# Softmax attention: maxima six pairs of heads ahead of the scores, their row fetched earlier and in one transfer

## The chip, the cores and the metric

The kernel runs on one core of one Trainium2 chip. The metric is the device time of one execution in microseconds. Three runs of the kernel before gave 2570.91, 2579.21 and 2582.12 us, median 2579.21 us. TensorE is called PE here, VectorE DVE, ScalarE ACT, GpSimd POOL and SyncE SP.

## The reference, cut to what matters

The program is four blocks, each added to the residual stream: softmax attention over the channels, a mixture of 8 experts, linear attention, and causal attention with a mixture of 16 experts. Only the first block is touched. There `x` and `ctx` are 64 sequences of 64 rows by 256 positions, cut into 32 tiles of two sequences.

```python
# _L0_xattn_ref, b = batch, 8 heads of 8 channels, 256 positions
q = split_heads(_proj(x, Wq, bq)); k = split_heads(_proj(c, Wk, bk)); v = split_heads(_proj(c, Wv, bv))
q = _apply_rotary(q_emb, q); k = _apply_rotary(k_emb, k)
scores = jnp.einsum('bhtc,bhsc->bhts', q, k) / math.sqrt(K_CH)
p_attn = jax.nn.softmax(scores, axis=-1)
out = jnp.einsum('bhts,bhsc->bhtc', p_attn, v)
```

## The kernel before, in words

`stage_softmax_attention` takes one tile per iteration of `for i in every`, and every engine has its own copy of that loop, in an order written out by hand; semaphores alone connect them. A tile has 16 heads (8 for each of its two sequences), worked on as 8 pairs, `k` = 0 to 7. Each pair needs two sets of products:

- Products for the maxima (`p_a`, L816). DVE reduces each of the pair's two heads to its largest score per query (`maxima`, L735), which goes into `top`.
- Scores themselves (`p_b`, L809), with the negative maximum taken off by an extra row (`SPLIT`, row 31 of each group of 32) of the same stationary block `rep`. ACT takes their exponential (L630).

`both(i, k)` (L791 to L819) issues the scores of pair `k` of tile `i` and, between them, the products for the maxima of a later pair. Before, that is four pairs on: pair `k + 4` of tile `i + 1` for `k` < 4, and pair `k - 4` of tile `i + 2` after that. Each half of `p_a` is written again only when DVE has reduced it (`a_done`), each half of `p_b` only when ACT has taken it (`prob_ready`).

Once all maxima of tile `i + 1` stand, PE turns them (L877) into `p_x[0]`, beside the v projection of tile `i + 3` (L881): call these six matmul records the turning block. ACT copies the turned row to `peak` (L664) and the values to `vaug` (L670), and SP sends the row to the four partitions 31, 63, 95 and 127 of `rep` (L543, four transfers). `both(i + 1, 0)` waits for them on `peak_in`.

Between the calls of `both` PE has other work: `project(i + 4, False)` after `k` = 0, `values(i - 1, 3)` and the router's `grade` (L211) after 1, `project(i + 4, True)` after 2, `values(i, 0)` after 3, the turning block after 4, `values(i, 1)` after 5, the output projection (L894) after 6, the router's `turn` (L193) and `values(i, 2)` after 7. `project` is L846 and L847; its True form waits for `cos_done`, that is for DVE's L721 on the False form. DVE's order is `maxima(i, 0)`, statistics of a later tile, `maxima(i, 1)`, rope with the cosines, `maxima` 2 and 3, rope with the sines, `maxima` 4 to 7, and then the reciprocal of the row sums (L782). The reciprocal waits for `pack_in`, the eight transfers of L592 that POOL issues.

SP's order in one iteration is: a blank store (L527), the twelve transfers that fill `rep` for tile `i + 3` (L504), the store of a finished tile (L537), the row of maxima (L543), loads (L518) and weights of the next stage (L402). The router works on tiles 0 to 15 only.

Of the kernel before, what the change touches and what calls it, by code (L numbers as in the profile page):

```python
# [20 lines left out]
PART = 128  # L21
# [18 lines left out]
def past(eng, sem, count):  # L40

    if not (isinstance(count, int) and count <= 0):
        eng.wait_ge(sem, count)
# [368 lines left out]
def stage_softmax_attention(nc, x_in, x_out, ctx, c):  # L412
# [15 lines left out]
    with st:  # L428
# [77 lines left out]
        with nc.Block() as block:  # L506
            @block.sync
            def _(sp):
                for dst, src in ((w_in, c["sa_w_in"]), (w_out, c["sa_w_out"]), (cos_t, c["sa_cos"]),
                                 (sin_t, c["sa_sin"]), (cols, c["sa_cols"]), (ident_f, c["ident"])):  # L510
                    sp.dma_start(dst[:], src).then_inc(const_in, 16)

                def load(m):
                    past(sp, xo_ready, LOAD * (m - 3))
                    past(sp, v_ready, LOAD * (m - 3))
                    at = slice(LOAD * (m % 4), LOAD * (m % 4) + LOAD)
                    for buf, src, done in ((xt, x_in, x_in_s), (ct, ctx, c_in_s)):
                        sp.dma_start(buf[:, at, :], src[LOAD * m:LOAD * (m + 1)].rearrange("t p d -> p t d")  # L518
                                     ).then_inc(done[m % 4], 16)

                load(0)
                load(1)
                route.load(sp)
                sp.wait_ge(zeroed, 2)
                for i in every:
                    if 0 <= i < len(blanks):
                        sp.dma_start(blanks[i].rearrange("(p r) d -> p (r d)", p=PART), blank[:]).then_inc(cleared[int(i >= CLEARS[0])], 16)  # L527
                    n = i + 3
                    if live(n):
                        sp.wait_ge(lo_ready, n + 1)  # L530
                        sp.wait_ge(hi_ready, n + 1)
                        sp.wait_ge(rep_init, min(n + 1, 4))
                        past(sp, b_ready, 2 * PAIRS * (n - 3))
                        fill_rows(sp, n, range(4 if n else 2))
                    if live(i - 3):
                        sp.wait_ge(xo_ready, i - 2)
                        sp.dma_start(x_out[i - 3], xo[:, (i - 3) % KEEP, :]).then_inc(stored[(i - 3) % KEEP], 16)  # L537
                    n = i + 1
                    if live(n):
                        sp.wait_ge(peak_ready, n + 1)  # L540
                        for j in range(4):
                            at = 32 * j + SPLIT
                            sp.dma_start(rep[at:at + 1, n % 4, :, 0:T].bitcast(fp32), peak[4 * j:4 * j + 4, n % 2, :].bitcast(fp32)  # L543
                                         ).then_inc(peak_in[n % 2], 16)
                    if (i + 9) % LOAD == 0 and 2 <= (i + 9) // LOAD < TILES // LOAD:
                        load((i + 9) // LOAD)
                    if i == 8:
                        held.load(sp)
                    if 0 <= i - 9 < held.RAWS:
                        held.load_raw(sp, c["L0_ffn_gate_proj"], c["L0_ffn_up_proj"], i - 9, i - 8)  # L550
                held.landed(sp)
                sp.wait_ge(route.wk_ready, route.TOP)
                sp.wait_ge(route.expert_ready, 1)
                for s in range(KEEP):
                    sp.wait_ge(stored[s], 16 * TILES // KEEP)
                sp.wait_ge(cleared[0], 16 * CLEARS[0])
                sp.wait_ge(cleared[1], 16 * (CLEARS[1] + MORE))
                sp.wait_ge(route.sent, 16 * route.n * route.TOP)
# [56 lines left out]
            def _(act):  # L615
# [23 lines left out]
                for i in every:  # L639
# [3 lines left out]
                    exp(i, 2)  # L643
                    keep(i - 1, 3)
                    exp(i, 3)
                    if routed(i - 6):
                        route.keep_scores(act, i - 6, 1, p_x[0][:, T:T + 8])
                    exp(i, 4)
                    keep(i, 0)
                    exp(i, 5)  # L650
                    n = i + 5
                    if live(n):
                        act.wait_ge(low_ready, n + 1)
# [2 lines left out]
                                       ).then_inc(xn_ready, 1)  # L656
                    if n in (0, 1, 2):
                        begin(n + 1)
                    n = i + 1
                    if live(n) or live(i + 3):  # L660
                        act.wait_ge(v_ready, i + 4)
                    if live(n):
                        past(act, peak_in[n % 2], 64 * (n // 2))
                        act.activation(peak[0:HEADS, n % 2, :], p_x[0][0:HEADS, T:2 * T], ACT.Copy).then_inc(peak_ready, 1)  # L664
                    n = i + 3
                    if live(n):
                        if n == 0:
                            act.wait_ge(zeroed, 5)
                        past(act, pv_done, GROUPS * (n - 3))
                        act.activation(vaug[:, n % 4, :, :, 0:KC].rearrange("p c h k -> p (c h) k"),  # L670
                                       p_x[0][:, 0:T].rearrange("p (n k) -> p n k", k=KC), ACT.Copy).then_inc(vaug_ready, 1)
                    exp(i, 6)
                    keep(i, 1)
                    exp(i, 7)
# [29 lines left out]
            def _(dve):  # L704
# [18 lines left out]
                                                 op0=ALU.add, op1=ALU.mult).then_inc(done, 1)  # L723

                def maxima(i, at):
                    n, k = (i + 1, at + 4) if at < 4 else (i + 2, at - 4)
                    if not live(n):
                        return
                    g, rows = pair(k ^ 1)
# [55 lines left out]
            def _(pe):  # L785
# [5 lines left out]
                def both(i, k):  # L791


                    n, m = (i + 1, k + 4) if k < 4 else (i + 2, k - 4)
                    if live(i) and k == 0:
                        pe.wait_ge(peak_in[i % 2], 64 * (i // 2 + 1))
                    if live(n) and m == 0:
                        pe.wait_ge(rep_in[n % 4], REP * (n // 4 + 1))
                    for h in range(2):
# [50 lines left out]
                for i in every:  # L850
# [1 line left out]
                    project(i + 4, False)  # L852
                    both(i, 1)
                    values(i - 1, 3)
                    if routed(i - 6):
                        route.grade(pe, i - 6, 1, p_x[0][:, T:T + 8], turned)

                    both(i, 2)
                    project(i + 4, True)
                    both(i, 3)  # L860
                    values(i, 0)

                    both(i, 4)
                    n, v = i + 1, i + 3
                    past(pe, vaug_ready, min(v, TILES))
                    past(pe, peak_ready, min(n, TILES))
                    past(pe, route.score_out, min(i - 5, ROUTED))
                    past(pe, route.ht_ready, min(i - 5, ROUTED))
                    if i > RANK:
                        pe.wait_ge(route.rank_out, 1)  # L870
# [11 lines left out]
                                           ct[:, v % RING, sc * PART:(sc + 1) * PART], w_in[:, 4, :], start=True, stop=True)  # L882
                    if mm is not None:
                        mm.then_inc(v_ready, 1)
                    both(i, 5)
                    values(i, 1)

# [8 lines left out]
                    if routed(i - 5) or i in (RANK, RANK + 1):  # L896
                        past(pe, vaug_ready, min(i + 4, TILES))
                        past(pe, peak_ready, min(i + 2, TILES))
                    if routed(i - 5):
                        route.turn(pe, i - 5, 1, p_x[0], ident_f[:])  # L900
                    if i == RANK:
# [1753 lines left out]
```

## Time and profile before

| | us |
|---|---|
| median of three runs | 2579.21 |
| the profiled execution | 2583.23 |
| span of that execution | 2581.4 |
| PE busy over the span | 2209.2 (86%) |
| DVE busy over the span | 1835.6 (71%) |
| ACT busy over the span | 1153.9 (45%) |

The span is 1.8 us shorter than the profiled execution. The first stage is the first 660 us of it. An instruction's row gives its start in us from the start of the span, how long it took, its engine, its line, its operation, what it writes and reads, how many are merged in the row, and in brackets how long the engine stood idle before it and what ended that idle time. One iteration runs from one first score product of pair 0 to the next. Idle time of an engine costs something only where the engines that set the end wait with it.

### The profile page before, as it was taken

Reading aid. Unit: us, or ns where it says so; the run is one execution under the profiler, and the core shown is the slowest. Engines: PE = TensorE matmul, PEld = TensorE weight load, DVE = VectorE, ACT = ScalarE, POOL = GpSimd, SP = SyncE. Lnnn points to the kernel's source line nnn. Section 1 sums busy time; section 2 is a strip of 40 time slices with the busy share of each in tenths; the row PEclk is TensorE's granted clock in tenths of the full one; section 3 lists DMA queues with packets and bytes.
Section 4 is the critical chain, followed back from the end, with each engine's and each line's share of the span. In section 5 each row is a group of like instructions: output and inputs, shape, how many; then the busy total and the mean of one; then the engine's idle time right before and its main releaser. Section 6 shows DMA issues by size and latency. Waiting matters only on the chain. (4 is left out here: it accounts for less than half of the span.)

```text
span 2581.4 us, 60448 instructions
## 1 busy us (share of the span) xinstructions
PE 2209.2 (86%) x20880; PEld 1675.0 (65%) x20880; DVE 1835.6 (71%) x3965; ACT 1153.9 (45%) x2509; POOL 1106.4 (43%) x1111
## 2 busy tenths in 40 slices
PE   6899888887678899994899998999988599999990
PEld 4555555543666677762677777777776477888880
DVE  4888888873546688765878878878787374545754
ACT  2776767665434333323444444444333264333330
POOL 3455554466144221002555445455487600334736
PEclk9988988886799999996999999999989799999995
DMA  5455554452359333312332332322334372445855
GB/s 114 120 124 137 147 136 129 104 144 85 120 171 296 110 107 120 92 58 53 82 89 57 83 84 60 85 73 69 81 96 116 129 253 82 136 141 182 264 172 148
DMA packets 250723, 313.10 MB, mean 121 GB/s; under 512 B 45248, under 2 KB 202944, under 8 KB 250432
## 3 DMA queue, kind: packets, MB, share of 16 engines
q1 hardware_dynamic: 189456, 219.11, 30.5%
q0 software_dynamic: 26624, 58.79, 8.3%
q10 hardware_dynamic: 34352, 31.34, 3.6%
q8 instruction: 180, 2.95, 0.5%
q14 instruction: 111, 0.91, 0.1%
HBM read 122.40 MB, written 102.24 MB: 87 GB/s over the span
## 5 line engine op out<-in xcount | busy, mean ns | idle before, releaser
L2136 POOL TENSOR_TENSOR ca_qk<-ca_qk,ca_q_swap 128x512 f32<-128x512 f32 x160 | 249.2, 1557 | 365.7 <-DVE ca_q_swap L2314 365.3
L735 DVE TENSOR_REDUCE soft_top<-soft_pa 128x2 fp32r<-128x512 f32 x512 | 327.9, 682 | 90.4 <-PE soft_pa L816 87.9
L630 ACT ACTIVATE soft_prob<-soft_pb 128x512 f32<-128x512 f32 x512 | 286.1, 594 | 180.9 <-PE soft_pb L809 179.1
L809 PE MATMUL soft_pb<-soft_rep 32*128 32x256 f32 x1024 | 207.5, 359 | 58.0 <-DVE soft_top L735 30.9
L809 PEld LDWEIGHTS soft_pb<-soft_rep 32*128 32x128 f32 x1024 | 135.0, 211 | 175.6 <-issue 81.3
L816 PE MATMUL soft_pa<-soft_rep 31*128 31x256 f32 x1024 | 217.4, 366 | 6.0 <-DVE soft_top L735 3.5
L1469 PE MATMUL moe_py<-moe_w_d,moe_at 128*128 x788 | 214.2, 387 | 1.5 <-issue 1.1
L1450 PE MATMUL moe_pgu<-moe_w_hi,moe_xt_hi 128*128 x472 | 192.9, 409 | 24.1 <-DVE moe_xt_lo L1362 13.4
L2406 PE MATMUL ca_py<-ca_w_hi,ca_ot_hi 128*128 128x256 f32 x512 | 155.8, 304 | 37.9 <-DVE ca_ot_lo L2335 37.8
L1368 DVE TENSOR_TENSOR moe_act_f<-moe_silu,moe_pgu 128x256 f32<-128x256 f32 (+1 forms) x236 | 88.6, 375 | 133.7 <-ACT moe_silu L1263 129.7
L2314 DVE TENSOR_TENSOR ca_q_swap<-ca_q_swap,ca_sin_q 128x512 f32<-128x512 f32 x128 | 116.8, 913 | 82.3 <-DMA ca_q_swap<-ca_q_f 81.9
L1263 ACT ACTIVATE moe_silu<-moe_pgu 128x256 f32<-128x256 f32 (+1 forms) x236 | 82.1, 348 | 203.9 <-PE moe_pgu L1450 203.7
L1450 PE MATMUL moe_pgu<-moe_w_hi,moe_xt_lo 128*128 x472 | 171.2, 363 | 0.0
L1450 PE MATMUL moe_pgu<-moe_w_lo,moe_xt_hi 128*128 x472 | 170.9, 362 | 0.0
L830 PE MATMUL soft_po<-soft_prob,soft_vaug 128*32 128x256 f32 x2048 | 164.0, 446 | 0.0
L2198 ACT ACTIVATE ca_ot_hi<-ca_po 128x512 fp32r<-128x512 f32 x128 | 69.5, 596 | 208.9 <-PE ca_po L2504 208.9
L2406 PE MATMUL ca_pp<-ca_ht_hi,ca_w_hi 128*128 128x512 f32 x312 | 138.2, 443 | 22.0 <-ACT ca_q_f L2184 18.4
L1184 POOL DMA_INDIRECT moe_yg<-moe_ys_rows,moe_held x112 | 115.8, 1034 | 87.7 <-DVE moe_ys L1375 38.5
L1362 DVE TENSOR_TENSOR moe_xt_lo<-moe_pt,moe_xt_hi 128x256 fp32r<-128x256 f32 x236 | 99.4, 421 | 72.8 <-ACT moe_xt_hi L1258 71.2
L2406 PE MATMUL ca_py<-ca_w_lo,ca_ot_hi 128*128 128x256 f32 x512 | 149.2, 291 | 0.0
L2406 PE MATMUL ca_py<-ca_w_hi,ca_ot_lo 128*128 128x256 f32 x512 | 149.1, 291 | 0.0
L364 POOL DMA_INDIRECT moe_rows<-moe_x_new,moe_held x80 | 78.1, 976 | 163.4 <-DVE moe_ys L1375 91.1
(377 smaller groups left out, 6265.7 us busy)
## 6 DMA issues: line engine op xcount, KB each, us to landing
ca_q_swap<-ca_q_f SPq DMA_DIRECT2D x640, 64.0 KB
moe_xs<-moe_rows SPq DMA_DIRECT2D x236, 128.0 KB, 2.1
soft_rep<-soft_parts SPq DMA_DIRECT2D x378, 64.0 KB
moe_rows<-soft_blank SPq DMA_DIRECT2D x27, 768.0 KB
moe_ys_rows<-moe_ys ACTq DMA_DIRECT2D x134, 128.0 KB
moe_ys<-moe_ys ACTq DMA_DIRECT2D x102, 128.0 KB
moe_xd<-scratch SPq DMA_DIRECT2D x64, 128.0 KB, 2.5
ca_vs<-ca_v SPq DMA_DIRECT2D x32, 256.0 KB, 3.9
```

What stands on the lines that cost most here:

```text
L630: act.activation(prob[:, k % 4, h, :], p_b[:, 2 * T * h:2 * T * (h + 1)], ACT.Exp).then_inc(prob_ready, 1)
L735: dve.tensor_reduce(heads[:, j, :, g], p_a[:, 2 * T * h:2 * T * (h + 1)].rearrange("p (c s) -> p c s", c=HALF), AX, ALU.max).then_inc(a_do ...
L809: mm = pe.matmul(p_b[:, out], rep[of, i % 4, g, at:at + PART], rep[of, i % 4, g, 0:T], start=True, stop=True)
L816: mm = pe.matmul(p_a[:, out], rep[of, n % 4, g, at:at + PART], rep[of, n % 4, g, T:2 * T], start=True, stop=True)
L830: mm = pe.matmul(p_o[g % 2][32 * j:32 * j + 32, 0:T], vaug[:, i % 4, sc, 4 * g + j, :], prob[:, (2 * g + j // 2) % 4, j % 2, sc * T:(sc + ...
L1184: pool.indirect_dma_start(out=yg[:, t % HELD, k, :], out_offset=None, in_=ys_rows[h], in_offset=bass.IndirectOffsetOnAxis(ap=slot_id[:, t, ...
L1362: dve.tensor_tensor(xt_lo[:, b % 2, :, :], p_t[b % 2][:, 0:DIM].rearrange("p (k t) -> p k t", k=KC), xt_hi[:, b % 2, :, :].bitcast(fp32), ...
L1450: mm = pe.matmul(p_gu[b % 2][:, 0:W2], x[:, b % 2, k, :], w, start=(n == 0), stop=(n == 3 * KC - 1))
L1469: mm = pe.matmul(p_y[b % 2][:, 0:DIM], at[:, b % 2, m, :], w_d[:, bass.ds(e, 1), m, :].rearrange("p a d -> p (a d)"), start=(m == 0), stop ...
L2136: pool.tensor_tensor(qk[:, u % 2, m, :], qk[:, u % 2, m, :], q_swap[:, p % 2, :], ALU.add).then_inc(qk_ready, 1)
L2314: dve.tensor_tensor(out.rearrange("p (b s) -> p b s", s=SEQ), src.rearrange("p (b s) -> p b s", s=SEQ), tab[int(m == RQ)][:].unsqueeze(1). ...
L2406: mm = pe.matmul(out, x, y, start=start and n == 0, stop=stop and n == len(todo) - 1)
```

## The change

The maxima run six pairs ahead. Pair `k + 6` of tile `i + 1` goes with `k` < 2, pair `k - 2` of tile `i + 2` with the rest. The turning block moves from after `both(i, 4)` to after `both(i, 2)`, ahead of `project(i + 4, True)`. ACT's copies of the row and of the values move from after the exponential of pair 5 to after that of pair 3. The router's grading of a tile moves from after `values(i - 1, 3)` to after `both(i, 4)`, and ACT's copy of its scores from after pair 3 to after pair 5. SP sends the row in one transfer, in the same place of its order.

```diff
                     n = i + 1
                     if live(n):
                         sp.wait_ge(peak_ready, n + 1)
-                        for j in range(4):
-                            at = 32 * j + SPLIT
-                            sp.dma_start(rep[at:at + 1, n % 4, :, 0:T].bitcast(fp32), peak[4 * j:4 * j + 4, n % 2, :].bitcast(fp32)
-                                         ).then_inc(peak_in[n % 2], 16)
+                        sp.dma_start(rep[SPLIT:PART:32, n % 4, :, 0:T].bitcast(fp32), peak[0:HEADS, n % 2, :].bitcast(fp32)
+                                     ).then_inc(peak_in[n % 2], 16)
...
                     exp(i, 3)
-                    if routed(i - 6):
-                        route.keep_scores(act, i - 6, 1, p_x[0][:, T:T + 8])
+                    n = i + 1
+                    if live(n) or live(i + 3):
+                        act.wait_ge(v_ready, i + 4)
+                    if live(n):
+                        past(act, peak_in[n % 2], 16 * (n // 2))
+                        act.activation(peak[0:HEADS, n % 2, :], p_x[0][0:HEADS, T:2 * T], ACT.Copy).then_inc(peak_ready, 1)
+                    n = i + 3
+                    if live(n):
+                        if n == 0:
+                            act.wait_ge(zeroed, 5)
+                        past(act, pv_done, GROUPS * (n - 3))
+                        act.activation(vaug[:, n % 4, :, :, 0:KC].rearrange("p c h k -> p (c h) k"),
+                                       p_x[0][:, 0:T].rearrange("p (n k) -> p n k", k=KC), ACT.Copy).then_inc(vaug_ready, 1)
                     exp(i, 4)
                     keep(i, 0)
                     exp(i, 5)
+                    if routed(i - 6):
+                        route.keep_scores(act, i - 6, 1, p_x[0][:, T:T + 8])
...
                 def maxima(i, at):
-                    n, k = (i + 1, at + 4) if at < 4 else (i + 2, at - 4)
+                    n, k = (i + 1, at + 6) if at < 2 else (i + 2, at - 2)
...
                 def both(i, k):
-                    n, m = (i + 1, k + 4) if k < 4 else (i + 2, k - 4)
+                    n, m = (i + 1, k + 6) if k < 2 else (i + 2, k - 2)
                     if live(i) and k == 0:
-                        pe.wait_ge(peak_in[i % 2], 64 * (i // 2 + 1))
+                        pe.wait_ge(peak_in[i % 2], 16 * (i // 2 + 1))
...
                     both(i, 1)
                     values(i - 1, 3)
-                    if routed(i - 6):
-                        route.grade(pe, i - 6, 1, p_x[0][:, T:T + 8], turned)
 
                     both(i, 2)
-                    project(i + 4, True)
-                    both(i, 3)
-                    values(i, 0)
-
-                    both(i, 4)
                     n, v = i + 1, i + 3
                     past(pe, vaug_ready, min(v, TILES))
                     past(pe, peak_ready, min(n, TILES))
-                    past(pe, route.score_out, min(i - 5, ROUTED))
+                    past(pe, route.score_out, min(i - 6, ROUTED))
...
                     if mm is not None:
                         mm.then_inc(v_ready, 1)
+                    project(i + 4, True)
+                    both(i, 3)
+                    values(i, 0)
+
+                    both(i, 4)
+                    if routed(i - 6):
+                        past(pe, vaug_ready, min(i + 4, TILES))
+                        past(pe, peak_ready, min(i + 2, TILES))
+                        route.grade(pe, i - 6, 1, p_x[0][:, T:T + 8], turned)
                     both(i, 5)
                     values(i, 1)
...
                     if routed(i - 5) or i in (RANK, RANK + 1):
                         past(pe, vaug_ready, min(i + 4, TILES))
                         past(pe, peak_ready, min(i + 2, TILES))
+                        past(pe, route.score_out, min(i - 5, ROUTED))
```

## Rows read from the trace of the kernel before

**Rows 1.** Stretches: length, busy us of each engine, granted clock, DMA share, GB/s.

```profile
77.20:595.30 518.10, 458.43 (x4286) 275.41 (x4286) 432.50 (x869) 356.74 (x769) 278.87 (x404) 0.88 0.52 130
320.60:337.20 16.60, 14.85 (x150) 9.16 (x150) 15.02 (x30) 13.13 (x30) 9.37 (x14) 1.00 0.56 137
509.80:525.10 15.30, 13.99 (x146) 8.46 (x146) 13.75 (x29) 11.85 (x25) 13.07 (x18) 1.00 0.55 166
429.00:448.50 19.50, 18.92 (x148) 10.84 (x148) 13.85 (x32) 11.66 (x26) 7.62 (x12) 0.65 0.30 76
```

**Rows 2.** Waits, 77 to 598 us: who for whom, total us, times, longest.

```profile
DVE soft_top L735 <- PE soft_pa L816: 72.7, 91, 4.4
...
PE soft_pb L809 <- DVE soft_top L735: 25.1, 39, 3.7
...
PE soft_pb L809 <- DMA soft_rep<-soft_peak: 16.7, 24, 2.7
...
DVE soft_rsum L782 <- DMA soft_sums<-soft_o_raw: 8.1, 9, 1.9
```

**Rows 3.** Timeline of DVE from 507 us, the iteration that starts at 509.78.

```profile
508.82 1.74 DVE L782 RECIPROCAL soft_rsum<-soft_sums 128x256 f32<-128x256 f32 x1
510.48 1.22 DVE L735 TENSOR_REDUCE soft_top<-soft_pa 128x2 fp32r<-128x512 f32 x2
...
514.33 1.28 DVE L735 TENSOR_REDUCE soft_top<-soft_pa 128x2 fp32r<-128x512 f32 x2
516.10 1.29 DVE L735 TENSOR_REDUCE soft_top<-soft_pa 128x2 fp32r<-128x512 f32 x2 [0.49 <-PE soft_pa L816]
...
521.52 2.67 DVE L735 TENSOR_REDUCE soft_top<-soft_pa 128x2 fp32r<-128x512 f32 x4 [0.77 <-PE soft_pa L816]
```

**Rows 4.** Timeline of PE, the same iteration.

```profile
509.78 0.38 PE L809 MATMUL soft_pb<-soft_rep 32*128 32x256 f32 x1 [0.61 <-DMA soft_rep<-soft_peak]
...
514.47 0.70 PE L846 MATMUL soft_px<-soft_xn,soft_w_in 128*128 128x256 f32 x2 [0.19 <-DVE soft_by_cos L721]
...
515.53 0.38 PE L809 MATMUL soft_pb<-soft_rep 32*128 32x256 f32 x1
...
517.97 0.44 PE L877 MATMUL soft_px<-soft_ident,soft_top 128*128 128x128 f32 x2
...
518.92 0.35 PE L809 MATMUL soft_pb<-soft_rep 32*128 32x256 f32 x1
```

**Rows 5.** Timeline of the SP queue, two iterations.

```profile
336.12 0.39 SPq L518 DMA_DIRECT2D soft_xt<-in_x  x1
...
510.66 9.96 SPq L504 DMA_DIRECT2D soft_rep<-soft_parts  x12
520.67 0.46 SPq L537 DMA_DIRECT2D scratch<-soft_xo  x1
521.38 2.53 SPq L543 DMA_DIRECT2D soft_rep<-soft_peak  x4
```

**Rows 6.** Timeline of POOL: the last of the eight transfers of an iteration.

```profile
347.57 0.60 POOL L592 DMA_DIRECT2D soft_sums<-soft_o_raw  x1
```

**Rows 7.** Timeline of DVE, 350 to 357 us.

```profile
354.44 1.75 DVE L782 RECIPROCAL soft_rsum<-soft_sums 128x256 f32<-128x256 f32 x1 [1.91 <-DMA soft_sums<-soft_o_raw]
356.68 0.69 DVE L735 TENSOR_REDUCE soft_top<-soft_pa 128x2 fp32r<-128x512 f32 x1 [0.48 <-PE soft_pa L816]
```

**Rows 8.** Timeline of PE, 29 to 60 us, the stage's start.

```profile
30.26 1.22 PE L846 MATMUL soft_px<-soft_xn,soft_w_in 128*128 128x256 f32 x2 [0.97 <-DVE soft_by_cos L721]
...
34.83 0.80 PE L816 MATMUL soft_pa<-soft_rep 31*128 31x256 f32 x4 [2.49 <-DMA soft_rep<-soft_parts]
...
55.77 1.39 PE L816 MATMUL soft_pa<-soft_rep 31*128 31x256 f32 x4 [0.78 <-DVE soft_top L735]
57.34 1.40 PE L816 MATMUL soft_pa<-soft_rep 31*128 31x256 f32 x4 [0.18 <-DVE soft_top L735]
59.01 0.55 PE L809 MATMUL soft_pb<-soft_rep 32*128 32x256 f32 x1 [0.27 <-DVE soft_top L735]
```

**Rows 9.** Groups by line: busy us and mean ns of the router's grading.

```profile
L211 PE MATMUL soft_px<-soft_r_router,soft_turned 128*128 128x8 f32 x64 | 11.8, 294 | 0.0
```

More of the change, by code:

```diff
@@ L658, in _ @@
                         begin(n + 1)
[L659 to L671, printed above, removed]
                     exp(i, 6)
```

## Prediction

> **What bounds the kernel now.** I first read the stretches by window, since the change touches only the first stage. Between the first score products of tiles 1 and 30 the stage spends 518.1 us, at a mean granted clock of 0.88 [rows 1]. Two kinds of iteration stand there. With the clock at 2.4 GHz throughout, one takes 16.6 us (with routing) or 15.3 us (without). Where the clock falls to 1.2 GHz for part of it, one takes 19.5 us. At 0.88 about (1 - 0.88) x 2 x 518 = 124 us run at 1.2 GHz, which touches about half of the iterations.
>
> The second view is the waits. PE waits 16.7 us in all for the row of maxima, 24 times [rows 2], and that is what the change goes for. But DVE is busy 13.75 of 15.3 us in a full-clock iteration, PE 13.99 [rows 1], so I asked which of the two the other waits for. The timeline answers. At 509.78 PE starts pair 0 after 0.61 us of waiting for the row [rows 4]. DVE meanwhile works on the reciprocal, which ends at 510.56, and takes up the reductions at 510.48 with no idle time [rows 3]. The row came late for PE and in time for DVE. From there DVE runs without a gap until 516.10, where it stood idle for 0.49 us, and it is idle once more, 0.77 us before 521.52 [rows 3]. These two gaps and the reciprocal's waits are nearly all that DVE loses at full clock, and none of them is ended by the row. So at full clock DVE and the chain through those two gaps set the pace, and PE's wait at the boundary lies beside the reciprocal (1.74 us). At 1.2 GHz PE sets the pace: 18.92 busy of 19.5 us [rows 1].
>
> One rule of the Trainium skill is weighed here. Perfetto Trace Analysis, section Identifying the Most-Contended Engine, says that matmul busy time is no measure of how near PE is to its limit, that the share of weight loads is the better one, and that for DVE occupancy is fair. The page would make PE's waits worth nothing at full clock, since weight loads fill only 8.46 of the 15.3 us [rows 1]. A reading by matmul busy time (13.99 against DVE's 13.75) would make them worth their 16.7 us. The sum below goes with the timeline, not with either figure.
>
> **The change part by part.**
>
> The row's wait. The turning block ends about two pairs sooner, and so does ACT's copy. SP, however, comes to the row only behind the fill (to 520.62) and the store (to 521.13), and in the same iteration it issued the row at 521.38 [rows 5]. So the issue itself moves by a quarter of a microsecond. What is saved is three of four issues, 3 x 0.63 = 1.9 us of the 2.53 [rows 5]. In the iteration shown, four issues ended at 523.91 and the next pair 0 started about 1.2 us later. One transfer of about 0.6 us from 521.13 should land near 523.0, two microseconds ahead of its use. The 24 waits should go. Their worth for the end is what DVE lost through them. The clearest case is the 0.48 us before 356.68 [rows 7]; a few iterations show something like it, most nothing. Bounds 0 and 16.7 us, taken 1.5 us, nearest to the row of DVE.
>
> The turning block's new place. It takes from 517.97 to 518.92, 0.95 us [rows 4]. Before, what stood between pairs 2 and 3 was the second projection alone, and PE waited 0.19 us there for the cosines. Now the block comes first, so the projection starts 0.95 - 0.19 = 0.76 us later. Pair 3 follows from 515.53 to about 516.3, and DVE, idle since 515.61, starts its reduction 0.76 us later: the gap of 0.49 becomes 1.25 us. Is it given back? The block is gone between pairs 4 and 5. But pair 5 of PE waits for DVE's reduction of pair 4, which is late by the same 0.76, so PE idles there instead. From pair 5 the way to DVE's second gap is unchanged: two half products, the values' products, pair 6. That gap stays 0.77 and the shift stays whole. Cost: 0.75 us for each full-clock iteration. Bounds: 0 (PE catches up through slack that I don't see) and 0.95. With 15 such iterations, 11.3 us. In the others PE is the bound, and an order of the same work costs little while it is slow; the rest of such an iteration runs at full clock. Taken 0.15 us x 14 = 2 us, bounds 0 and 0.75 each.
>
> The grading. Its 64 products take 11.8 us over 16 tiles, 0.7 us each [rows 9]. Its new place, ahead of pair 5, is just where PE now idles 0.8 us for DVE, so it is hidden. Its old place was hidden too, by DVE's statistics. Taken 0; if the cover is gone it costs 0.7 x 16 = 11 us. ACT's moved copies (two, between pairs 3 and 4) fall where ACT waits for PE, taken 0. The extra wait before the router's turn is met an exponential earlier, taken 0.
>
> What gives back. The reciprocal waits for POOL's transfers nine times, 8.1 us in all [rows 2]. The last one issued at 347.57 ended its wait only at 354.44 [rows 6, 7], so they land by their own time. When the reductions end 0.75 us later, that much of each wait goes. Nine waits, at most 0.75 each, some shorter: -4 us, bounds 0 and -6.8.
>
> The two ends of the stage. Before the first scores, two more pairs of maxima must be done, at 1.57 us a pair (57.34 less 55.77) [rows 8]: 3.1 us. A projection (its first half takes 1.22 us at 30.26, the whole about 2.1) that stood ahead of the wait for the first fill (34.83) [rows 8] now stands behind the first product, and PE and DVE are both short of work there: 2.1 us. In the next iteration the block and the projection fall together between two reductions, about 1.2 us more, an estimate from the 0.95 above at the slower clock. So the first scores start about 6.4 us after 59.01. At the far end, two pairs of scores lose the maxima beside them; they save between 0 and 2 x 1.57, taken 1.5. Ends: +4.9 us, bounds 1 and 7.
>
> Sum: 11.3 + 2 - 4 + 4.9 - 1.5 = 12.7, rounded to 12 us for the covers that I may have missed. The profiled execution of before took 2583.2 us (span 2581.4 and 1.8 around it), so 2595 by its measure. It lies 4.0 us above the median of the three runs, 2579.2. Beside that median the forecast is 2591 us, 0.46% more.
>
> **The rivals.**
>
> A. PE is the bound after all, and its 16.7 us go: 2562.5 us. For it: in slow iterations PE is busy 18.92 of 19.5 us. Against it: DVE is not idle behind the wait.
>
> B. The clock falls less often. A slow iteration costs 19.5 - 16.6 = 2.9 us more [rows 1]. A longer lead evens out PE's work at the boundary; four fewer slow iterations take 12 us off the forecast: 2579. For it: the boundary is where PE stands still longest, and 1.2 GHz stretches begin near it. Against it: the wait for DVE takes the row's place there.
>
> C. The clock falls more often. Pairs 2 and 3 now have 0.95 us more between them and PE idles 0.8 us at pair 5. Six more slow iterations: 2591 + 6 x 2.9 = 2608.
>
> D. Bulk transfers collide with the sums. The loads, weights and blank stores stand behind the row in SP's queue (336.12) [rows 5]; they now go out two to three microseconds sooner, while POOL's transfers are still on their way (347.57 to 354.44). If each reciprocal is 1 us later in 28 iterations, 28 us: 2619. It decides once the sums land more than 0.75 us later than now. The DMA page of the Trainium skill (DMA: Bandwidth & Descriptors, section Issuing engines are not separate DMA queues) says that transfers of all issuing engines run on the same 16 engines and interleave; by that rule the collision is real, though it names no price for it here.
>
> E. The row's wait stays, because the one transfer lands late behind the fill. The cost of the order remains: 2592.
>
> **How the numbers follow.** The forecast gets 0.45, A 0.12, B 0.14, C 0.12, D 0.12, E 0.05. The forecast's own range is 2583 to 2601. A change of 0.5% (12.9 us, limits 2566.3 and 2592.1) is about what a measurement of this kernel can tell from none. The forecast lies just inside, so I split it: 0.25 within, 0.20 above. A is faster; B is within, with 0.03 faster; C and D are slower; E is within. That gives faster 0.15, same 0.41, slower 0.44. The range of 2570 to 2611 reaches into B and C and leaves out most of A and D.
>
> **What would show it.** PE's wait for the row should be gone from the list of waits. DVE's gap before the reduction of pair 3 should be about 1.2 us at full clock instead of 0.49, with the gap before pair 6 still near 0.77, and PE should wait for DVE about 0.8 us at pair 5 where nothing is graded. A full-clock iteration without routing should take about 16.0 us instead of 15.3. The first scores should start near 65 us. The forecast is wrong if the gap before pair 3 stays near 0.5 us, or if the mean granted clock between tiles 1 and 30 moves away from 0.88 by more than 0.02, or if the reciprocal's wait grows.

## The result, and the profile after

The changed kernel takes 2623.26 us (median of 4 runs, 2617.41 to 2626.46) where the kernel before takes 2579.89 (4 runs). The ratio is 1.018 with a 95% interval of 1.0149 to 1.0208. It is slower by 43 us, outside the predicted range of 2570 to 2611.

The profiled execution after took 2626.5 us, before 2583.2. All of the difference is in the first stage: its last score product ends at 678.0 us, before at 632.3, that is 45.7 us later (the rest of the program takes 2.4 us less). Inside the stage it goes as follows. The first scores start at 64.90 instead of 59.01 (5.9 us). The iteration of tile 0 takes 2.9 us more (21.1 against 18.2). Tiles 1 to 30 take 38.9 us more (557.0 against 518.1). The last two iterations take 2.0 us less. So the question is tiles 1 to 30.

The first view is the same as in [rows 1], by windows, now of the kernel after: the whole stretch of tiles 1 to 30, two parts of one iteration (6.6 and 6.9 us), and one iteration at full clock.

```profile
86.01:642.99 556.98, 498.02 (x4292) 292.40 (x4288) 451.31 (x870) 357.61 (x769) 278.39 (x404) 0.77 0.51 121
185.00:191.60 6.60, 6.11 (x69) 3.86 (x67) 5.70 (x10) 4.69 (x13) 5.67 (x9) 1.00 0.72 107
191.60:198.50 6.90, 6.45 (x48) 3.47 (x44) 5.37 (x8) 4.83 (x10) 0.50 (x1) 0.51 0.46 145
389.15:405.65 16.50, 14.74 (x156) 9.06 (x152) 14.27 (x29) 12.20 (x28) 9.41 (x14) 0.99 0.46 120
```

The granted clock of tiles 1 to 30 fell from 0.88 to 0.77. Worked as in the prediction, that is (1 - 0.77) x 2 x 557 = 256 us at 1.2 GHz, where before had 124. It is not a matter of the one execution that was profiled: over the whole program the four runs after have a clock of 0.887 to 0.901, and the 73 runs of the kernel before that were taken beside the experiments 0.907 to 0.931. The second and third rows show how it looks in one iteration: full clock until 191.6, then 1.2 GHz. Between 80 and 600 us the record of the granted clock has 26 such stretches after and 14 before, most of them 6.8 us long, so almost every iteration has one now. The last of the 26 begins at 597.8 and lasts to 679.8: the last full iterations run at 1.2 GHz throughout (19.8 and 19.6 us), where before the last one started at 598.4 and took in only the two tiles of the end. The last row is the rare iteration (tile 17) that ran at full clock: 16.50 us with routing, against 16.60 before (tile 15) [rows 1]. In this one pair of iterations the new order costs nothing; more of them are compared below.

The second view is the list of waits after, 77 to 640 us.

```profile
DVE soft_top L733 <- PE soft_pa L814: 102.3, 110, 3.0
...
PE soft_pb L807 <- DVE soft_top L733: 45.2, 67, 3.2
...
DVE soft_rsum L780 <- DMA soft_sums<-soft_o_raw: 0.3, 1, 0.3
```

PE no longer waits for the row of maxima at all: the 16.7 us of [rows 2] are gone, and the wait for the sums fell from 8.1 to 0.3. PE's wait for DVE grew by 20 us, DVE's for PE by 30. What the change went for was reached, and the two engines wait for each other more.

The third view is the timeline of DVE after, in the iteration that starts at 179.2, and with it the one instruction of POOL that matters.

```profile
184.69 1.28 DVE L733 TENSOR_REDUCE soft_top<-soft_pa 128x2 fp32r<-128x512 f32 x2
186.88 1.29 DVE L733 TENSOR_REDUCE soft_top<-soft_pa 128x2 fp32r<-128x512 f32 x2 [0.90 <-PE soft_pa L814]
...
190.06 1.45 DVE L760 SCALAR_TENSOR_TENSOR soft_low<-soft_mv,soft_rstd 128x1 f32<-128x1 f32 x1
```

```profile
190.14 1.34 POOL L598 TENSOR_TENSOR soft_roped<-soft_by_cos,soft_by_sin 128x512 f32<-128x512 f32 x1
```

The gap ahead of the reduction of pair 3 is 0.90 us; it was 0.49 [rows 3], and 1.25 was predicted. On PE the emptied place shows at pair 5, where it now waits for DVE: 0.34 us where a tile is graded there, 0.88 where none is.

```profile
495.68 0.35 PE L807 MATMUL soft_pb<-soft_rep 32*128 32x256 f32 x1 [0.88 <-DVE soft_top L733]
```

The surprise is `low`, one number per partition, which took 1.45 us. It ends with POOL's addition `roped` (191.51 and 191.48). Here is the same place in the kernel before.

```profile
331.38 0.15 DVE L762 SCALAR_TENSOR_TENSOR soft_low<-soft_mv,soft_rstd 128x1 f32<-128x1 f32 x1
```

```profile
331.87 1.35 POOL L600 TENSOR_TENSOR soft_roped<-soft_by_cos,soft_by_sin 128x512 f32<-128x512 f32 x1
```

Before, `low` started 0.49 us ahead of `roped` and took 0.15. After, DVE is 0.90 - 0.49 = 0.41 us later against POOL, and the lead is 0.08. By groups of lines, 26 of these instructions each (total us, mean ns), first after (80 to 640 us), then before (77 to 598 us):

```profile
L760 DVE SCALAR_TENSOR_TENSOR soft_low<-soft_mv,soft_rstd 128x1 f32<-128x1 f32 x26 | 28.6, 1100 | 0.0
```

```profile
L762 DVE SCALAR_TENSOR_TENSOR soft_low<-soft_mv,soft_rstd 128x1 f32<-128x1 f32 x26 | 11.6, 446 | 0.0
```

The collision was there before in some iterations (`low` took over 0.3 us in 7 of the 26). Now it is in most of them (23 of 26), and DVE loses 17.0 us more to it. The Trainium skill, SBUF — State Buffer, section Who interferes with whom, says that a DVE instruction with two SBUF inputs contends with a GpSimd instruction that reads SBUF, and that issue order decides which of the two is blocked. The first half agrees with the 1.45 us beside `roped`. The second half doesn't agree by the records: `low` started 0.08 us first and it was the one that waited. The start of a record may not be the moment of issue; no run here shows that moment.

### The profile page after: what moved, and what is told of

It reads as the page before. It is cut to its first block and busy times, and to the rows that moved or that the text cites. A ratio compares the mean times of both kernels' runs of the same rounds, so it can differ in the third digit from the quotient of the medians.

```text
span 2624.7 us, 60381 instructions
## 1 busy us (share of the span) xinstructions
PE 2250.2 (86%) x20880; PEld 1694.8 (65%) x20880; DVE 1856.2 (71%) x3965; ACT 1155.1 (44%) x2509; POOL 1105.5 (42%) x1111
## 5 line engine op out<-in xcount | busy, mean ns | idle before, releaser
L807 PE MATMUL soft_pb<-soft_rep 32*128 32x256 f32 x1024 | 225.7, 395 | 58.8 <-DVE soft_top L733 47.3
L807 PEld LDWEIGHTS soft_pb<-soft_rep 32*128 32x128 f32 x1024 | 147.0, 238 | 198.2 <-issue 118.4
L814 PE MATMUL soft_pa<-soft_rep 31*128 31x256 f32 x1024 | 234.7, 401 | 9.8 <-DMA soft_rep<-soft_parts 5.2
L828 PE MATMUL soft_po<-soft_prob,soft_vaug 128*32 128x256 f32 x2048 | 184.1, 491 | 0.0
L814 PEld LDWEIGHTS soft_pa<-soft_rep 31*128 31x128 f32 x1024 | 150.0, 237 | 16.3 <-DVE soft_top L733 6.3
```

Source lines behind the costliest of these rows:

```text
L807: mm = pe.matmul(p_b[:, out], rep[of, i % 4, g, at:at + PART], rep[of, i % 4, g, 0:T], start=True, stop=True)
L814: mm = pe.matmul(p_a[:, out], rep[of, n % 4, g, at:at + PART], rep[of, n % 4, g, T:2 * T], start=True, stop=True)
L828: mm = pe.matmul(p_o[g % 2][32 * j:32 * j + 32, 0:T], vaug[:, i % 4, sc, 4 * g + j, :], prob[:, (2 * g + j // 2) % 4, j % 2, sc * T:(sc + ...
```

## The experiments

My theory at this point: (1) the clock falls in every iteration because PE has too little to do around pairs 4 and 5, where the turning block used to be; (2) `low` collides with `roped`. The rivals: that the lead of six pairs or the one transfer itself costs the time; that the collision causes the falls as well; that the new order costs what I had predicted. The kernels ran in three groups, and each ratio is to the kernel before on the same chip. Medians of before were 2576.45, 2576.16 and 2572.82 us.

**First group: each suspect by itself.**

`after_low_behind_5` moves `low` one reduction later in DVE's order.

```diff
                     maxima(i, 4)
+                    maxima(i, 5)
                     if live(new):
                         dve.wait_ge(rstd_ready, new + 1)
                         dve.scalar_tensor_tensor(out=low[:], in0=mv[:, 0:1], scalar=-1.0, in1=rstd[:],
                                                  op0=ALU.mult, op1=ALU.mult).then_inc(low_ready, 1)
-                    maxima(i, 5)
                     maxima(i, 6)
```

> The kernel after, with one DVE instruction moved: the 128x1 product that makes `low` (L760) goes from behind maxima 4 to behind maxima 5. In the trace of after it takes 1.43 us (median) and ends with POOL's addition `roped` in 18 of 26 iterations; in before it takes 0.15 us. Theory 1, the collision of these two instructions comes first and the falls of the clock follow from it: low falls to under 0.5 us mean, the stage's iterations to about 17 us, the granted clock of the stage rises, total 2585 to 2600 us. Theory 2, the new order of PE's work makes the clock fall and the collision lies beside it: low is short, but the total stays within 8 us of after, 2615 to 2625 us. Theory 3, both, independent: 22 iterations x 1.3 us = 28 us less, 2595 us, with the clock unchanged at 0.79 in 80 to 600 us.

Measured: 2605.93 us (4 runs), ratio 1.0110 (1.0053 to 1.0168), 17 us below the changed kernel. `low` has a median of 150 ns. But the clock between 80 and 600 us is 0.81 (0.79 after, 0.88 before), with 22 falls. The third theory comes nearest, with 2595 us against 2606: the collision is part of the loss, and the falls stay without it.

`before_six_old_order` is the kernel before with the one transfer and the lead of six pairs; the turning block, the grading and ACT's copies stay where they were.

```diff
-                    n, m = (i + 1, k + 4) if k < 4 else (i + 2, k - 4)
+                    n, m = (i + 1, k + 6) if k < 2 else (i + 2, k - 2)
...
-                        for j in range(4):
-                            at = 32 * j + SPLIT
-                            sp.dma_start(rep[at:at + 1, n % 4, :, 0:T].bitcast(fp32), peak[4 * j:4 * j + 4, n % 2, :].bitcast(fp32)
+                        sp.dma_start(rep[SPLIT:PART:32, n % 4, :, 0:T].bitcast(fp32), peak[0:HEADS, n % 2, :].bitcast(fp32)
```

> The kernel before with the maxima six pairs ahead and the row in one transfer; the turning block stays behind pair 4, grading and ACT's copies stay. Theory 1 (order of the block shifts DVE onto POOL's addition): DVE's order in time is as before, low stays at about 0.4 us mean, total 2584 us, which is before plus about 5 us for the stage's two ends. Theory 2 (six pairs ahead are themselves bad): 2600 us or more.

Measured: 2578.93 us (10 runs), ratio 0.9995 (0.9968 to 1.0023). The lead of six pairs costs nothing measurable, and brings nothing; the interval leaves 8 us to one side and 6 to the other.

`before_one_transfer` has the second half of that diff alone.

> The kernel before with the row of maxima in one transfer and nothing else changed. The transfers of the row end 1.9 us sooner, PE's wait for the row falls from 16.7 us to under 3 us. If PE's wait lies beside the reciprocal, as predicted, the total is within 4 us of before (2576 to 2584 us). If PE's wait counts, 2565 us.

Measured: 2571.22 us (10 runs), ratio 0.9985 (0.9955 to 1.0016). PE's wait for the row fell from 16.7 us to 4.0, and no time came of it that stands clear of the noise (4 us by the ratio). The row was late for PE and hardly for the stage.

`before_low_behind_3` takes `low` out of reach of `roped` in the kernel before, ahead of the sines instead of behind `maxima(i, 4)`.

```diff
                     maxima(i, 3)
-                    rope(i + 4, True)
-                    maxima(i, 4)
                     if live(new):
...
                                                  op0=ALU.mult, op1=ALU.mult).then_inc(low_ready, 1)
+                    rope(i + 4, True)
+                    maxima(i, 4)
```

> The kernel before with the product `low` moved from behind maxima 4 to behind maxima 3. In before it meets POOL's addition in 9 of 26 iterations and takes 11.6 us in all. Theory 1: it is then short everywhere and the total falls by 3 to 8 us (2572 to 2577 us), more if falls of the clock go with it. Rival: from tile 20 on POOL makes rstd late and DVE waits for it at the new place, up to 0.4 us in 8 iterations, and nothing is gained.

Measured: 2568.24 us (10 runs), ratio 0.9960 (0.9931 to 0.9988); `low` is never above 161 ns. The kernel before paid for the collision too, about 8 to 10 us (medians, ratio), at an unchanged clock of 0.89.

The clock and the busy times of these kernels, and of the second group, stand in one view by windows, 80 to 600 us. In order: before, after, `after_low_behind_5`, then `before_six_old_order`.

```profile
80.00:600.00 520.00, 457.52 (x4291) 275.09 (x4290) 433.97 (x869) 357.21 (x770) 279.75 (x405) 0.88 0.51 129
```

```profile
80.00:600.00 520.00, 464.25 (x4037) 273.92 (x4030) 427.02 (x837) 336.31 (x725) 257.59 (x375) 0.79 0.51 120
```

```profile
80.00:600.00 520.00, 467.01 (x4177) 276.71 (x4169) 417.62 (x854) 347.76 (x749) 269.07 (x390) 0.81 0.52 126
```

```profile
80.00:600.00 520.00, 459.61 (x4384) 276.64 (x4385) 435.26 (x876) 364.95 (x788) 288.85 (x418) 0.89 0.53 133
```

The instructions (x) tell how much work was done in the 520 us: 4037 matmul records after, 4291 before. PE's busy time hides this, since matmuls last longer at 1.2 GHz (one score product takes 0.35 us at 189.70 and 0.55 at 192.26, behind the fall): it is higher after (464) than before (458).

**Second group: the clock.**

`after_low5_filled` is `after_low_behind_5` with spare products ahead of pair 5, three where a tile is graded and seven elsewhere. They multiply the identity matrix by itself, 128x256, into a half of `p_o[1]` that nobody reads at that time, and do nothing for the result.

```diff
+                    for _ in range(count):
+                        pe.matmul(p_o[1][:, T:2 * T].rearrange("p (c k) -> p c k", c=2), ident[:],
+                                  ident[:].unsqueeze(1).to_broadcast([PART, 2, PART]), start=True, stop=True)
...
+                    spare(0 if not live(i) else 3 if routed(i - 6) else 7, GROUPS * i)
                     both(i, 5)
```

> The kernel after_low_behind_5 with extra PE products ahead of pair 5, where PE waits for DVE: identity times identity, 128 rows, 256 columns, fp32r, into an unused half of p_o, 7 where nothing is graded and 3 where the router grades (beside the 4 graded). Nobody reads them. Theory 1, the clock falls because PE does too little around pairs 4 and 5: with the slot filled the falls behind it stop, the granted clock of 80 to 600 us goes from 0.81 to 0.87 or more, the total from 2606 to 2575 to 2590 us, although PE has more to do. Theory 2, the falls come from the longer block of other work between pairs 2 and 3 or from the boundary: the clock stays at 0.81 and the total rises by 0 to 10 us.

Measured: 2578.36 us (10 runs), ratio 1.0015 (0.9992 to 1.0038). By adding work to PE the kernel became some 24 us faster than `after_low_behind_5` (ratio 1.0015 against 1.0110). Its window, and then one iteration of it at full clock (tile 21):

```profile
80.00:600.00 520.00, 456.33 (x4499) 280.56 (x4495) 432.05 (x880) 361.07 (x783) 282.82 (x408) 0.93 0.53 130
426.79:442.11 15.32, 14.61 (x155) 8.96 (x152) 13.47 (x29) 11.90 (x27) 8.86 (x13) 1.00 0.52 125
```

The clock is at 0.93, with 11 falls. Between 80 and 600 us the records show 139 spare products with a mean of 308 ns, 24.6 us of PE's busy time. DVE's gap at pair 3 is still 0.90 us here, so DVE being late does not by itself make the clock fall; what changed is that PE no longer waits at pair 5.

`after_low5_v_back` has no spare work. It is `after_low_behind_5` with only the turned row left at its new place: the v projection goes back behind pair 4, ACT's copy of the values behind the exponential of pair 4, and the grading behind `values(i, 1)`.

```diff
-                    if live(v):
-                        for sc in range(HALF):
-                            mm = pe.matmul(p_x[0][:, sc * PART:(sc + 1) * PART],
...
                     both(i, 4)
+                    if live(v):
+                        past(pe, peak_ready, min(i + 2, TILES))
+                        for sc in range(HALF):
+                            mm = pe.matmul(p_x[0][:, sc * PART:(sc + 1) * PART],
...
+                        mm.then_inc(v_ready, 1)
+                    both(i, 5)
+                    values(i, 1)
                     if routed(i - 6):
...
-                    both(i, 5)
-                    values(i, 1)
```

> The kernel after_low_behind_5 with the v projection (L872, four of the six records of the turning block) back behind pair 4, and ACT's copy of the values behind pair 4; only the maxima are turned early. The grading goes behind values 1. Theory 1, too little work of PE around pairs 4 and 5: clock 0.86 or more in 80 to 600 us and 2575 to 2590 us. Also the 0.90 us gap of DVE ahead of the reduction of pair 3 should fall to about 0.5. Theory 2, the early turning itself is to blame: clock 0.81 and 2600 us or more.

Measured: 2570.75 us (10 runs), ratio 0.9983 (0.9963 to 1.0003), and this window:

```profile
80.00:600.00 520.00, 450.02 (x4392) 272.32 (x4392) 438.89 (x877) 366.17 (x790) 288.91 (x418) 0.92 0.54 133
```

DVE's gap at pair 3 is back at 0.49, as expected, though the row is still turned early; and PE waits 0.23 us at pair 5:

```profile
257.80 1.29 DVE L733 TENSOR_REDUCE soft_top<-soft_pa 128x2 fp32r<-128x512 f32 x2 [0.49 <-PE soft_pa L814]
```

Four products of work that the kernel does anyway, put back between pairs 4 and 5, bring the clock back as well as spare ones do. This ties the falls to an edit of the change: not to the lead, nor to the transfer, nor to the turned row's earlier turn, but to the v projection (and the grading and ACT's copy, which moved with it and were not tried apart). `low` collides in part here (mean 519 ns), and still the kernel is no slower than before.

`before_low3_one` joins `before_low_behind_3` and the one transfer.

> The kernel before with both edits that helped or did no harm alone: the row in one transfer and `low` behind maxima 3. If they add: 2576.5 - 8 - 5 = 2563 us. If only `low` counts: 2568 us.

Measured: 2568.32 us (10 runs), ratio 0.9977 (0.9952 to 1.0002). The transfer adds nothing to what `low` brought.

`before_low3_one_filled` adds four spare products to that, between `both(i, 0)` and `project(i + 4, False)`.

```diff
                     both(i, 0)
+                    spare(4 if live(i) else 0, GROUPS * (i - 1) + 2)
                     project(i + 4, False)
```

> before_low3_one with four such extra PE products at the start of each iteration, between pair 0 and the first projection, where PE stands idle while DVE takes its reciprocal. If the falls of the clock in the kernel before come from this slot, the granted clock of 80 to 600 us rises from 0.88 to 0.93 or more and the total falls by 8 to 20 us below before_low3_one. If not, PE only has more to do: 0 to 8 us above it.

Measured: 2562.33 us (9 runs, 2550.81 to 2568.91), ratio 0.9945 (0.9919 to 0.9971). It is the fastest of all, 14 us below the kernel before and, by the ratios, 60 below the changed one. Against `before_low3_one` it is 6 to 8 us faster, a little less than expected, and the two intervals overlap. The clock rose from 0.88 to 0.92, with spare work at another place of the iteration than pair 5. So spare work that raises the clock does not alone show where the falls come from; `after_low5_v_back`, which adds none, shows it better. The window of `before_low3_one_filled`:

```profile
80.00:600.00 520.00, 471.07 (x4540) 287.66 (x4539) 429.22 (x875) 368.20 (x794) 290.88 (x421) 0.92 0.53 133
```

**Third group: the collision by itself, and the rest.**

`after_filled_low_kept` is the changed kernel with the spare products of `after_low5_filled` and `low` left where the change had it. It completes a square of two suspects.

> The kernel after with the extra PE products ahead of pair 5 (7 or 3, as in after_low5_filled), but with `low` left behind maxima 4, where it meets POOL's addition. With `low` moved as well the total was 2578 us, without the products 2606 us, without both 2623 us. If the collision costs DVE about 1.28 us in each iteration once the clock holds, the total is 2578 + 22 x 1.28 = 2606 us. If the collision counts mainly because it helps the clock to fall, it is 2578 to 2590 us.

Measured: 2587.59 us (5 runs), ratio 1.0056 (1.0034 to 1.0077). The clock of 80 to 600 us is 0.90, with 14 falls: the spare work holds it also where `low` collides. Its `low`:

```profile
L760 DVE SCALAR_TENSOR_TENSOR soft_low<-soft_mv,soft_rstd 128x1 f32<-128x1 f32 x26 | 27.6, 1062 | 0.0
```

| ratio to the kernel before (median, us) | `low` collides | `low` moved |
|---|---|---|
| no spare work | 1.0179 (2623, the change) | 1.0110 (2606) |
| spare work ahead of pair 5 | 1.0056 (2588) | 1.0015 (2578) |

The four were not measured in one group, so I take the ratios, at 2578 us: 46, 28, 14 and 4 us above before. The falls that the spare work stops are worth 32 us with the collision and 24 without it. The collision is worth 18 us while the clock falls and 10 or 11 while it holds. The interval of 1.0110 leaves some 15 us on either side, so the 24 and the 18 are rough; those of the lower row leave 8 us on either side of the 10 or 11. Together they take 42 of the 46. I had expected about 2606 for this kernel, that is a bigger share for the collision; that was wrong, and the clock is the bigger part.

`before_dve_work_ahead` puts a spare `bn_stats` of 0.42 us ahead of `low` in the kernel before, to delay `low` against POOL as the change does. `before_dve_work_behind` puts the same instruction behind `low` instead. The diff is that of the first; `spare` is a buffer of its own that nobody reads.

```diff
                     if live(new):
+                        dve.bn_stats(spare[:], cos_t[:, 0:T]).then_inc(spare_done, 1)
+                    if live(new):
                         dve.wait_ge(rstd_ready, new + 1)
```

> The kernel before with a spare bn_stats of 128x256 (0.42 us) on DVE ahead of `low`, so that `low` starts 0.42 us later, as POOL's addition begins. Collision theory: `low` goes from 0.45 to over 1.1 us mean, the total to 2595 to 2610 us. If the collision is only a coincidence of the after kernel, the price is that of the spare work, at most 0.42 x 28 = 12 us, 2580 to 2588 us.

> The same spare bn_stats, but behind `low`: the same work for DVE without the delay of `low`. Collision theory: `low` stays near 0.45 us mean or below, the total rises by 0 to 12 us, to 2576 to 2588 us, and lies 15 us or more below before_dve_work_ahead. Rival, that 0.42 us of DVE work alone breaks the rhythm: both kernels take the same.

Measured: 2593.94 us (4 runs), ratio 1.0074 (1.0050 to 1.0098), and 2588.36 (4 runs), ratio 1.0061 (1.0037 to 1.0085). `low` of the one and of the other:

```profile
L765 DVE SCALAR_TENSOR_TENSOR soft_low<-soft_mv,soft_rstd 128x1 f32<-128x1 f32 x26 | 18.0, 692 | 0.0
```

```profile
L763 DVE SCALAR_TENSOR_TENSOR soft_low<-soft_mv,soft_rstd 128x1 f32<-128x1 f32 x26 | 13.7, 529 | 0.0
```

The second expectation was a distance of 15 us or more between the two, and they lie 3 to 6 apart: by these numbers the rival, that the work alone costs the time, did better. The pair is weak as a test of the collision. The delay brought more collisions (692 ns against 529), but only a few of the 26, and the intervals overlap. In the kernel with the work ahead, `low` took 1.55 us in seven iterations, where it started 0.17 us before `roped`; in the others POOL's order had moved as well. What the pair does show is that 0.42 us more of DVE in each of 32 iterations, 13.3 us in all, costs 16 to 19 us by the ratios. That fits the prediction, in which DVE is in the chain that sets the pace. But the clock fell too, to 0.85 and 0.87 between 80 and 600 us (19 and 17 falls), so the price is not that of DVE's work alone.

`after_v_back_low3_filled` joins what had helped: `after_low5_v_back`, `low` behind `maxima(i, 3)`, and four spare products behind pair 0.

> The kernel after_low5_v_back with `low` behind maxima 3, where POOL is not adding, and with four extra PE products between pair 0 and the first projection, as in before_low3_one_filled. after_low5_v_back took 2571 us with `low` at 0.52 us mean: the shorter `low` is worth up to 0.37 x 26 = 10 us, the filling up to 6 us as in the kernel before. Forecast 2556 to 2562 us. Rival: PE and ACT share the pace there, and it stays at 2565 to 2571 us.

Measured: 2567.69 us (12 runs), ratio 0.9985 (0.9966 to 1.0004), a miss; 2556 to 2562 was expected. The clock was at 0.92 without the spare work and is 0.92 with it, so there was nothing for it to mend. It also stays 0.4% (10 us, give or take 8) behind `before_low3_one_filled`, whose ratio is 0.9945: with the same two remedies the old order is still the faster one.

## Why the prediction was wrong

By its steps:

- **The row's wait** was right. The wait is gone, and it was worth next to nothing: 0.9985 (0.9955 to 1.0016) for the one transfer alone. Rival A, which gave it 16.7 us, is refuted. The reading that led there (late for PE, in time for DVE) holds.
- **The turning block's new place** was right in kind and too big in size. Predicted was a gap of 1.25 us at pair 3 and 0.75 us for each full-clock iteration, 11.3 in all. The gap measured 0.90, so DVE is 0.41 us later and not 0.76; with the v projection back at its old place it is 0.49 again. Whole iterations can be compared where both kernels ran at full clock and `low` collides in neither. Between `before_low3_one` and `after_low5_filled` that is 13 tiles: from 0.52 us less to 0.55 more, median 0.33 more. Against `before_low_behind_3` it is ten tiles, with a median of 0.08. So the cost is some 0.1 to 0.3 us, less than half of the 0.75 taken, and small beside the spread of single iterations (`after_low5_filled` has its spare products in it as well).
- **The gap before pair 6 and PE's wait at pair 5** were right: a gap of 0.77 at 402.40 in tile 17, and a wait of 0.88 us where nothing is graded, 0.34 where something is. The grading is hidden.
- **The sums' wait** gave back 7.8 us instead of 4. That is no separate gain: DVE simply came later.
- **The ends of the stage**: 5.9 us at the first scores (6.4 predicted), -2.0 at the far end (-1.5). The iteration of tile 0 with 2.9 us was not in the sum.
- **The clock** is the step that failed; the sum has no term for it. "In the others PE is the bound, and an order of the same work costs little" assumed that the number of falls stays. Rival C named the right mechanism, at the right place ("PE idles 0.8 us at pair 5"), but gave it six more slow iterations and a chance of 0.12. There were twelve more falls; at the 2.9 us a piece worked out in the prediction that is 35 us, and the experiments measured 24 to 32. For six I had no reason; I had not asked what PE's slot between pairs 4 and 5 holds once the block has left it. The sign given for the failure of the forecast, a clock away from 0.88 by over 0.02, came true with 0.77.
- **The collision of `low` with `roped`** was missing altogether, 10 to 18 us. The trace of before showed it, with `low` at 0.15 us in most iterations and up to 1.86 in others. I never looked at the longest of a group of such short instructions, and so I did not ask what a DVE later by 0.4 us would run into on POOL.

The cause of the 43 us is therefore shown by taking each part away: with both gone the changed kernel takes 2578 us, 0.15% from before. That does not make the new order free. The kernel before pays for the collision too, and without it (`before_low3_one`, 0.9977, measured beside `after_low5_filled`, 1.0015) it is 10 us faster than the changed kernel without both, give or take 9. In the traces of these two the first scores start at 65.01 us against 58.13 and the last end at 628.0 against 622.3, so most of this remainder is the later start that the prediction had in its sum.

What stays open is why the clock falls there. In the row 185.00:191.60 PE is busy 6.11 of 6.60 us right before it falls, and no wait of PE in it is longer than 0.34. The runs show that more products around pair 5 stop most falls, not by what rule. Also not separated: whether the v projection alone, or ACT's copy and the grading with it, makes the difference in `after_low5_v_back`.

## What to carry to other kernels

Before moving work on PE, look at where the granted clock falls now and what stands in front of it; a slot that is emptied can cost more through the clock than the work in it was ever worth, and spare products in it are a cheap test. Compare matmuls done per microsecond, not PE's busy time, when the clock differs. For tiny instructions on DVE read the maximum as well as the mean, and if it is ten times the median, ask which instruction of POOL ends with it before shifting either engine.

## What the runs showed of the hardware that I had not expected

- A DVE instruction on 128x1 with two SBUF inputs takes 0.15 us alone and 1.45 beside POOL's addition of 1.34 us. It ends 0.03 us behind the addition, also where it starts 0.08 us (here) or 0.17 us (`before_dve_work_ahead`) ahead of it. With a lead of about 0.49 us it mostly ran freely (331.38 before), but not always: with 0.48 it took 1.86 us once (261.25 before), and with 0.58 once 1.96 (97.83 after). So the kernel before stood near the collision, and the recorded lead alone does not tell who waits.
- Adding 160 products of 0.3 us, of no use to the result, took a kernel from a ratio of 1.0110 to 1.0015, with the clock from 0.81 to 0.93.
- One transfer of 16 rows to partitions 31, 63, 95 and 127 took SP 0.56 us to issue, against 2.53 us for four [rows 5]. In the timeline of SP after:

```profile
189.76 0.56 SPq L541 DMA_DIRECT2D soft_rep<-soft_peak  x1
```
